# The split of q and k moves from DVE to POOL, attend's sums get a PSUM bank of their own, and every engine's order of work in a tick is written anew

## The chip, the cores and the metric

One core of one Trainium2 chip. The metric is device time in microseconds (us) of one execution; a run's time is the median of its executions. The trace is of one execution taken by the hardware profiler.

## The reference

16 batches of 128 tokens with 128 features go through three attention layers of 16 heads (8 features each) and an MLP:

```python
# layer CROSS0: adaptive layer norm of x and of the context (scale and shift from silu(cond) @ W)
q = (ada(x) @ Wq + bq); k, v = split(ada(ctx) @ Wkv + bkv)
x = x + softmax(q @ k.T / sqrt(8)) @ v @ Wp + bp
# layer SELF1: q, k, v from modulate(ln(x)); the result is gated per batch
x = x + gate_a * (attention(modulate(ln(x))) @ W_proj + b_proj)
# layer CROSS1: q from ln(x), k and v from ln(context); no gate
x = x + attention(ln(x), ln(context)) @ W_cproj + b_cproj
# MLP of 512 hidden features
x = x + gate_m * (gelu(modulate(ln(x)) @ W_mlp1 + b1) @ W_mlp2 + b2)
```

All inputs and outputs are fp32.

## The kernel before, in words

**Units and ticks.** A unit is one batch of one layer: 48 units, 16 for each layer. Four units make a group, 12 groups. Each engine runs a program that is written out in Python: a prologue for group 0, then a loop over ticks (from `FIRST` to `LAST`), and in each tick the steps of several units at different depths of a pipeline. The order of the steps in a tick is fixed by hand (or by a tool that wrote it) for each engine by itself; the engines meet only at semaphores. `front(tick, step)` gives the group whose steps are due at a tick: group g comes at tick 4g + step. So the steps that are done once for a group fall in one tick of every four. This text calls the tick classes T0, T1, T2, T3 by tick modulo 4.

**The steps of a unit.** `scores` (L495): eight bf16 matmuls in two row tiles of 62 rows write four head pairs' scores into `score_ps` (two banks, one buffer); c = 0 and 1 are the two halves of the heads, 0 and 1 in names below. DVE's `row_max` (L930) reduces them to negated maxima. POOL's `split_max` (L1098, L1100) makes two bf16 parts of these, PE's `turn_max` (L502) transposes them, DVE's `copy_max_rows` (L939) takes them to SBUF and SP moves them by two DMAs into the two spare rows of `stack_q` (`move_max`, L343). `keyed_scores` (L518) then computes the scores again, transposed and less their maxima, into `keyed_ps` (one buffer of two banks); ACT's `exponentials` (L737) make `probs`; `attend` (L532), 16 fp32 matmuls with 32 weight columns, multiplies with the values and sums; ACT's `copy_summed` (L745) takes the result out, `turn_summed` (L543) transposes it, DVE's `divide` (L945, L949) divides by the sums, `turn_attn` (L548), ACT's `attn_with_bias` (L754), `project_out` (L555) and DVE's `add_branch` (L960, L963) follow. POOL adds the output bias ahead (`add_out_bias`, L1127) or, in SELF1, multiplies by the gate and adds (`add_gated`, L1148, L1150).

**The steps of a group.** DVE's `norm_stats` (L893, L895), POOL's `inverse_root` (L1082 to L1090), ACT's `normalise_act` (L703) for x and DVE's `normalise` for the context, `transpose_normed` (L459), ACT's `modulate` (L689; plain copies in CROSS1, L682), `project_qk` (L469, one for q and one for k), `project_v` (L478), `copy_values`. q and k are needed as three bf16 parts each, whose sum is the fp32 value. ACT's `first_part` (L717) writes the first part from PSUM, DVE's `leave_rest` (L922) computes PSUM + bias − first part into the fp32 tile `rest`, and POOL's `split_rest` makes the second part by a cast (L1111) and the third by a subtraction (L1113). SP moves the parts by 12 DMAs of 128 KB for each group (`move_parts`, L322) into `stack_q` and `stack_k`; k's parts must have landed before `scores` of the group's first unit, three ticks ahead of the unit's own tick.

**PSUM.** `score_ps` and `keyed_ps` take two banks each; the other four are one ring ("all"), taken in the order that `at_tick` lists. `take` makes PE wait until the use four before has been read.

The MLP's steps (`mlp_up`, `leave_hidden`, `activate_hidden`, `mlp_down`, `add_mlp`) stand at ticks given by tables (`UP_AT`, `GELU_AT`, `DOWN_AT`, `ADD_AT`).

## Time and profile before

| | |
|---|---|
| median of 3 runs | 303.6 us (303.12 to 304.59) |
| the profiled execution | 304.21 us, of it a span of 302.4 us |
| PE matmuls busy | 264.3 us, 87% |
| DVE busy | 220.0 us, 73% |
| ACT busy | 221.8 us, 73% |
| POOL busy | 135.6 us, 45% |
| granted TensorE clock, mean | 0.977 |

The span is the time from the first to the last instruction in the trace; the profiled execution's own time is 1.8 us longer. Busy shares are averages over a start (about 45 us, with loads), the ticks with attention, and a tail (from about 250 us) with the MLP; from 70 to 250 us the granted clock is full.

### The profile page before, as it was taken

What the parts mean: (1) busy time and instruction counts of PE and PEld (TensorE: products, weight loads), DVE (VectorE), ACT (ScalarE), POOL (GpSimd) and SP (SyncE); (2) the same over time, 40 slices, a digit from 0 to 9 for tenths busy, and PEclk for the clock granted to TensorE, in tenths of its full rate; (3) what the DMA queues carried; (4) which work ended last, traced back from release to release, by engine and by line L of the source; (5) the groups of instructions that cost most, each with busy time, mean ns of one, the idle gap of its engine ahead of it and who ended that gap; (6) DMA issues with size and microseconds to landing.
All of it is one profiled execution on the core that took longest, in us unless ns stands there. A gap on an engine that the chain in (4) does not pass through costs nothing.

```text
span 302.4 us, 10123 instructions
## 1 busy us (share of the span) xinstructions
PE 264.3 (87%) x3811; PEld 172.7 (57%) x3811; DVE 220.0 (73%) x452; ACT 221.8 (73%) x399; POOL 135.6 (45%) x285
## 2 busy tenths in 40 slices
PE   2837679989899998989999999999999999978995
PEld 2523446656555665555656666566665555544875
DVE  7776867978778787787887988889878787322323
ACT  5345396886977869778687786976878879899940
POOL 8410924726346163253664735757248153160500
PEclk9975989999999999999999999999999999999999
DMA  6096985235433455432423234232442200000111
GB/s 199 3 208 178 189 189 136 69 89 135 114 108 96 124 131 112 108 112 77 110 69 95 69 95 108 59 95 69 108 108 56 57 5 4 4 2 0 35 54 52
DMA packets 34223, 27.44 MB, mean 91 GB/s; under 512 B 4904, under 2 KB 33920, under 8 KB 34176
## 3 DMA queue, kind: packets, MB, share of 16 engines
q1 hardware_dynamic: 32678, 25.54, 33.3%
q10 hardware_dynamic: 1498, 1.26, 1.7%
q8 instruction: 31, 0.51, 0.7%
q14 instruction: 16, 0.13, 0.1%
HBM read 6.46 MB, written 1.06 MB: 25 GB/s over the span
## 4 chain that ended last, share of the span: by engine, by line
PE 45%; DVE 15%; ACT 13%; POOL 9%; issue 9%; DMA 5%; SPq 3%; ACTq 1%; POOLq 0%; DVEq 0%
PE all_ps L469 8%; PE all_ps L532 8%; DVE neg_max L930 8%; PE score_ps L495 6%; ACT normed L703 4%; PE keyed_ps L518 4%; PE all_ps L543 4%; PE all_ps L459 3%; PE all_ps L563 3%; POOL rstd L1082 3%; PE all_ps L574 2%; PE all_ps L555 2%; ACT parts L717 2%; POOL parts L1113 2%; DMA stack_q<-max_rows 2%
## 5 line engine op out<-in xcount | busy, mean ns | idle before, releaser
L930 DVE TENSOR_REDUCE neg_max<-score_ps 128x8 f32<-128x1024 f32 x96 | 117.0, 1219 | 17.8 <-PE score_ps L495 17.8
L737 ACT ACTIVATE probs<-keyed_ps 128x1024 f32<-128x1024 f32 x96 | 98.2, 1022 | 18.0 <-PE keyed_ps L518 18.0
L532 PE MATMUL all_ps<-probs,values 128*32 128x128 f32 x1536 | 61.7, 280 | 0.3 <-ACT probs L737 0.3
L532 PEld LDWEIGHTS all_ps<-probs,values 128*32 128x32 f32 x1536 | 36.5, 109 | 19.9 <-issue 10.4
L495 PE MATMUL score_ps<-stack_k,stack_q 62*128 62x128 bf16 x768 | 38.6, 221 | 10.6 <-DVE neg_max L930 7.0
L518 PE MATMUL keyed_ps<-stack_q,stack_k 64*128 64x128 bf16 x768 | 38.0, 218 | 2.1 <-DMA stack_q<-max_rows 1.4
L495 PEld LDWEIGHTS score_ps<-stack_k,stack_q 62*128 62x128 bf16 x768 | 22.0, 95 | 30.4 <-DVE neg_max L930 17.3
L1098 POOL CAST max_parts<-neg_max 128x16 bf16<-128x16 f32 x48 | 9.7, 202 | 60.5 <-DVE neg_max L930 60.5
L745 ACT ACTIVATE summed<-all_ps 128x256 f32<-128x256 f32 x48 | 18.2, 380 | 19.1 <-PE all_ps L532 19.1
L469 PE MATMUL all_ps<-normed_t,w_qk 128*128 128x512 f32 x48 | 30.9, 739 | 0.0
L1082 POOL TENSOR_TENSOR rstd<-var_eps,minus_half 128x4 f32<-128x4 f32 x24 | 24.4, 1015 | 12.8 <-DVE var_eps L895 12.7
L518 PEld LDWEIGHTS keyed_ps<-stack_q,stack_k 64*128 64x128 bf16 x768 | 22.7, 94 | 12.8 <-issue 9.3
L1127 POOL TENSOR_TENSOR x_bias<-xs,b_out 128x128 f32<-128x128 f32 x32 | 14.7, 458 | 29.8 <-DVE xs L963 29.5
L1113 POOL TENSOR_TENSOR parts<-rest,parts 128x512 bf16<-128x512 f32 x23 | 26.6, 1155 | 1.8
L703 ACT ACTIVATE normed<-xs,offset,rstd 128x128 f32<-128x128 f32 x56 | 23.0, 485 | 5.9 <-POOL offset L1090 5.7
L922 DVE SCALAR_TENSOR_TENSOR rest<-all_ps,bcol_p,parts 128x512 f32<-128x512 f32 x24 | 17.9, 746 | 12.6 <-ACT parts L717 11.7
L1111 POOL CAST parts<-rest 128x512 bf16<-128x512 f32 x23 | 14.0, 609 | 25.0 <-DVE rest L922 25.0
L543 PE MATMUL all_ps<-ident,summed 128*128 128x128 f32 x96 | 20.9, 300 | 3.9 <-ACT summed L745 3.7
L963 DVE TENSOR_TENSOR xs<-all_ps,x_bias 128x128 f32<-128x128 f32 x32 | 9.2, 287 | 19.0 <-PE all_ps L555 17.9
L717 ACT ACTIVATE parts<-all_ps,bcol_p 128x512 bf16<-128x512 f32 x24 | 16.5, 689 | 7.7 <-PE all_ps L469 7.4
L459 PE MATMUL all_ps<-ident,normed 128*128 128x128 f32 x96 | 16.2, 295 | 5.3 <-DVE normed L907 3.7
L689 ACT ACTIVATE normed_t<-all_ps,mod 128x128 f32<-128x128 f32 x44 | 17.3, 462 | 4.1 <-PE all_ps L459 3.9
(103 smaller groups left out, 403.6 us busy)
## 6 DMA issues: line engine op xcount, KB each, us to landing
stack_q<-parts SPq DMA_DIRECT2D x72, 128.0 KB, 2.5
stack_k<-parts SPq DMA_DIRECT2D x66, 128.0 KB, 2.5
gate<-gate_d SPq DMA_DIRECT2D x16, 128.0 KB, 3.4
stack_q<-max_rows SPq DMA_DIRECT2D x96, 4.0 KB
xs<-in_x_dram SPq DMA_DIRECT2D x4, 256.0 KB, 3.0
cs<-in_ctx_dram SPq DMA_DIRECT2D x4, 256.0 KB, 3.5
out_dram<-xs SPq DMA_DIRECT2D x8, 128.0 KB, 1.8
stack_k<-parts ACTq DMA_DIRECT2D x6, 128.0 KB, 4.0
```

Source lines behind the costliest of these rows:

```text
L459: mm = pe.transpose(ps[:, j * T:(j + 1) * T], normed[:, n, j, :], ident[:, :])
L469: pe.matmul(take("qk"[n], g), w_qk[:, s, n, :], normed_t[:, src, :, :], start=True, stop=True).then_inc(qk_ps, 1)
L495: mm = pe.matmul(score_ps[:, e, a * T:(a + 1) * T], stack_q[rows, g % STACKS, CP * c + a, cols], stack_k[rows, g % STACKS, CP * c + a, col ...
L518: mm = pe.matmul(keyed_ps[:, e, a * T:(a + 1) * T], stack_k[rows, g % STACKS, CP * c + a, cols], stack_q[rows, g % STACKS, CP * c + a, col ...
L532: mm = pe.matmul(ps[QUAD * a:QUAD * (a + 1), c * T:(c + 1) * T], values[:, u // PER % STACKS, u % PER * PAIRS + CP * c + a, 2 * e:2 * e + ...
L543: mm = pe.transpose(ps[:, i * 128:(i + 1) * 128], summed[:, u % 2, i, :], ident[:, :])
L703: ins = act.activation(normed[:, n, j, :], src[:, b0 + j, :], ACT.Identity, bias=offset[:, n, j:j + 1], scale=rstd[:, n, j:j + 1])
L717: act.activation(parts[:, g % 2, n, 0, :], bank("qk"[n], g), ACT.Identity, bias=bcol_p[:, r:r + 1]).then_inc(hi_ready, 1)
L737: act.activation(probs[:, n % 3, :], keyed_ps[:, :, :].rearrange("t e n -> t (e n)"), ACT.Exp, scale=float(D) ** -0.5).then_inc(probs_read ...
L930: dve.tensor_reduce(neg_max[:, u % 2, :, CP * c:CP * (c + 1)], score_ps[:, :, :].rearrange("t e (a k) -> t e a k", k=T), AX.X, ALU.max, ne ...
L1082: ins = pool.tensor_tensor(rstd[:, n, :], var_eps[:, n, :], minus_half[:, :], ALU.pow)
L1113: pool.tensor_tensor(parts[:, g % 2, n, 2, :], rest[:, n, :], parts[:, g % 2, n, 1, :], ALU.subtract).then_inc(done, 1)
```

## The change

Four things change together.

- `leave_rest` goes (except for group 0). ACT's new `whole_part` writes q or k whole, in fp32, into `rest`; it waits until the part splitting of the group before is done. POOL's `split_rest` has four instructions in place of two: cast to the first part (L1127 in the new numbering), subtract it from `rest` in place with fp32 output (L1129), cast to the second (L1133), subtract for the third (L1135). SP waits for `hi_cast` (POOL) where it waited for `hi_ready` (ACT).
- The ring of four banks becomes one bank for `attend` ("way_in") and a ring of three for the rest.
- `max_parts` grows to 128 columns, of which 96 are zeros set once at the start; `turn_max` loads 128 weight columns in place of 32 and writes 128 rows, of which 32 are read.
- Each engine's order within a tick and the ticks of many steps are new; the loop runs from tick −7 to 57 in place of −6 to 56.

```diff
-RINGS = (("all", 4),)
+RINGS = (("way_in", 1), ("all", 3))
-        max_parts = sb("max_parts", [T, 2, 2, 2, PAIRS], BF16)
+        max_parts = sb("max_parts", [T, 2, 4, 2, 2, PAIRS], BF16)
-        FIRST = -6
-        LAST = 57
-        UP_AT = (40, 42, 43, 44, 44, 44, 45, 47, 48, 48, 48, 49, 52, 52, 52, 52)
-        DOWN_AT = (49, 50, 52, 52, 52, 53, 55, 55)
-        GELU_AT = (48, 49, 52)
-        ADD_AT = (51, 51, 52, 52, 52, 53, 53, 53)
+        FIRST = -7
+        LAST = 58
+        UP_AT = (41, 42, 43, 44, 45, 46, 48, 49, 49, 49, 50, 51, 54, 54, 54, 55)
+        DOWN_AT = (48, 51, 52, 53, 56, 56, 57, 57)
+        GELU_AT = (47, 49, 51)
+        ADD_AT = (48, 50, 51, 51, 51, 55, 55, 57)
...
+            def whole_part(g, n):
+                s = layer(g)
+                if g >= 2:
+                    act.wait_ge(split_ready, 2 * (2 * (g - 1) + n - 1))
+                else:
+                    act.wait_ge((q0_split, k0_split)[n], 2)
+                act.wait_ge(qk_ps, 2 * g + n + 1)
+                r = (R_Q, R_K)[n][s]
+                act.activation(rest[:, n, :], bank("qk"[n], g), ACT.Identity,
+                               bias=bcol_p[:, r:r + 1]).then_inc(whole_ready, 1)
...
             def split_rest(g, n):
-                pool.wait_ge(rest_ready, m + 1)
+                if g == 0:
+                    pool.wait_ge(rest_ready, m + 1)
+                else:
+                    pool.wait_ge(whole_ready, m - 1)
+                    if g >= 2:
+                        (q_in_place, k_in_place)[n](pool, g - 2)
+                    pool.tensor_copy(parts[:, g % 2, n, 0, :], rest[:, n, :]).then_inc(hi_cast, 1)
+                    pool.wait_ge(hi_cast, m - 1)
+                    pool.tensor_tensor(rest[:, n, :], rest[:, n, :], parts[:, g % 2, n, 0, :],
+                                       ALU.subtract).then_inc(rest_left, 1)
+                    pool.wait_ge(rest_left, m - 1)
                 pool.tensor_copy(parts[:, g % 2, n, 1, :], rest[:, n, :]).then_inc(done, 1)
```

**The new orders in words.** PE: scores 0, keyed 0, attend 1 of the unit before, turn_attn, [T1: q; T2: v; T0: transposes of x], scores 1, keyed 1, attend 0, turn_max, [T0: transposes of the context; T1: k], turn_summed, project_out. ACT: exponentials 0, copy_summed, [T2: copy_values], attn_with_bias, [T0: modulate x; T1: whole q], exponentials 1, [T0: half of modulate context; T1: whole k; T3: normalise_act], [T0: the other half]. DVE: row_max 0, add_branch (one tick later than before), [T1: normalise context], row_max 1, [T2: norm_stats], copy_max_rows, divide. POOL: out bias or gate, [T1: split of q; T2: split of k], split_max, [T2: inverse_root]. SP: [T2: q's parts; T3: the late parts of k], move_max, [T2: the first parts of k].

**PE, a plain tick and its neighbours, by the order of the instruction streams.** Before, layer CROSS0, from a tick's scores 0 to the next tick's:

```order
L495 MATMUL score_ps<-stack_k,stack_q 128x128 x8
L532 MATMUL all_ps<-probs,values 32x128 x8
L518 MATMUL keyed_ps<-stack_q,stack_k 128x128 x8
L555 MATMUL all_ps<-wp,attn_t 128x128
L502 MATMUL all_ps<-ident_b,max_parts 32x128
L543 MATMUL all_ps<-ident,summed 128x128 x2
L495 MATMUL score_ps<-stack_k,stack_q 128x128 x8
L518 MATMUL keyed_ps<-stack_q,stack_k 128x128 x8
L469 MATMUL all_ps<-normed_t,w_qk 128x512
L548 MATMUL all_ps<-ident,attn 128x128
L532 MATMUL all_ps<-probs,values 32x128 x8
L495 MATMUL score_ps<-stack_k,stack_q 128x128 x8
```

After, the same engine in tick T1 (scores are L498 now, keyed L523, attend L537, turn_attn L553, q and k L472, turn_max L507, turn_summed L548, project_out L560):

```order
L498 MATMUL score_ps<-stack_k,stack_q 128x128 x8
L523 MATMUL keyed_ps<-stack_q,stack_k 128x128 x8
L537 MATMUL way_in_ps<-probs,values 32x128 x8
L553 MATMUL all_ps<-ident,attn 128x128
L472 MATMUL all_ps<-normed_t,w_qk 128x512
L498 MATMUL score_ps<-stack_k,stack_q 128x128 x8
L523 MATMUL keyed_ps<-stack_q,stack_k 128x128 x8
L537 MATMUL way_in_ps<-probs,values 32x128 x8
L507 MATMUL all_ps<-ident_b,max_parts 128x128
L472 MATMUL all_ps<-normed_t,w_qk 128x512
L548 MATMUL all_ps<-ident,summed 128x128 x2
L560 MATMUL all_ps<-wp,attn_t 128x128
```

Both scores now stand directly before keyed scores, attend follows them, and all steps with 128 weight columns stand together after attend; q and k are in one tick.

**ACT, from the end of a T3 to the first exponentials of T1.** Before (SELF1 fronts; the normalising step stood in T2, the modulation in T3):

```order
L703 ACTIVATE normed<-xs,offset,rstd 128x128 x4
L745 ACTIVATE summed<-all_ps 128x256
L737 ACTIVATE probs<-keyed_ps 128x1024
L689 ACTIVATE normed_t<-all_ps,mod 128x128 x2
L737 ACTIVATE probs<-keyed_ps 128x1024
L689 ACTIVATE normed_t<-all_ps,mod 128x128 x2
```

After (exponentials are L755, copy_summed L763, attn_with_bias L772, modulate L694, normalise_act L708):

```order
L708 ACTIVATE normed<-xs,offset,rstd 128x128 x4
L755 ACTIVATE probs<-keyed_ps 128x1024
L763 ACTIVATE summed<-way_in_ps 128x256
L772 ACTIVATE attn_t<-all_ps,bcol 128x128
L694 ACTIVATE normed_t<-all_ps,mod 128x128 x4
L755 ACTIVATE probs<-keyed_ps 128x1024 x2
```

All four modulations now stand ahead of exponentials 1 of T0, where two stood ahead of it and two behind.

**POOL, T1 to T2, after, layer SELF1's fronts** (before, L1111 and L1113 alone made the split, L1098 and L1100 stood ahead of it):

```order
L1127 CAST parts<-rest 128x512
L1129 TENSOR_TENSOR rest<-rest,parts 128x512
L1133 CAST parts<-rest 128x512
L1135 TENSOR_TENSOR parts<-rest,parts 128x512
L1112 CAST max_parts<-neg_max 128x2x8
L1114 TENSOR_TENSOR max_parts<-neg_max,max_parts 128x2x8
L1095 TENSOR_TENSOR rstd<-var_eps,minus_half 128x4
```

The maxima's split and, in T2, the inverse root stand behind the four instructions of the k split.

## Rows read from the trace of the kernel before

**Rows 1.** Timeline, PE, start and us: the scores that open ticks 1, 9, 41, 44.

```profile
46.35 0.47 PE L495 MATMUL score_ps<-stack_k,stack_q 62*128 62x128 bf16 x8
...
86.01 0.40 PE L495 MATMUL score_ps<-stack_k,stack_q 62*128 62x128 bf16 x8
...
239.67 0.40 PE L495 MATMUL score_ps<-stack_k,stack_q 62*128 62x128 bf16 x8
...
253.60 0.40 PE L495 MATMUL score_ps<-stack_k,stack_q 62*128 62x128 bf16 x8
```

**Rows 2.** Timeline, PE weight loads of ticks 16 and 17: start, us, idle before.

```profile
119.56 0.23 PEld L495 LDWEIGHTS score_ps<-stack_k,stack_q 62*128 62x128 bf16 x8 [0.53 <-DVE neg_max L930]
119.89 0.38 PEld L532 LDWEIGHTS all_ps<-probs,values 128*32 128x32 f32 x16
120.47 0.23 PEld L518 LDWEIGHTS keyed_ps<-stack_q,stack_k 64*128 64x128 bf16 x8 [0.20 <-issue]
120.80 0.30 PEld L555 LDWEIGHTS all_ps<-wp,attn_t 128*128 128x128 f32 x2
121.21 0.09 PEld L502 LDWEIGHTS all_ps<-ident_b,max_parts 128*32 128x32 bf16 x1
121.37 0.20 PEld L543 LDWEIGHTS all_ps<-ident,summed 128*128 128x128 f32 x2
121.74 0.23 PEld L495 LDWEIGHTS score_ps<-stack_k,stack_q 62*128 62x128 bf16 x8 [0.17 <-issue]
121.98 0.23 PEld L518 LDWEIGHTS keyed_ps<-stack_q,stack_k 64*128 64x128 bf16 x8
...
125.28 0.30 PEld L469 LDWEIGHTS all_ps<-normed_t,w_qk 128*128 128x128 f32 x2
...
126.56 0.09 PEld L502 LDWEIGHTS all_ps<-ident_b,max_parts 128*32 128x32 bf16 x1
```

**Rows 3.** Timeline, DVE, a T2: maxima 0, then the steps up to maxima 1.

```profile
188.40 1.21 DVE L930 TENSOR_REDUCE neg_max<-score_ps 128x8 f32<-128x1024 f32 x1
189.53 0.28 DVE L960 TENSOR_TENSOR branch<-all_ps,b_out 128x128 f32<-128x128 f32 x1
...
190.34 1.22 DVE L930 TENSOR_REDUCE neg_max<-score_ps 128x8 f32<-128x1024 f32 x1
```

**Rows 4.** Timeline, ACT, a T2: exponentials, then normalise_act.

```profile
171.30 1.02 ACT L737 ACTIVATE probs<-keyed_ps 128x1024 f32<-128x1024 f32 x1 [0.49 <-PE keyed_ps L518]
...
172.47 1.64 ACT L703 ACTIVATE normed<-xs,offset,rstd 128x128 f32<-128x128 f32 x4
```

**Rows 5.** Groups by line and shape: busy us, mean ns; idle before, releaser.

```profile
L1113 POOL TENSOR_TENSOR parts<-rest,parts 128x512 bf16<-128x512 f32 x23 | 26.6, 1155 | 1.8
...
L1082 POOL TENSOR_TENSOR rstd<-var_eps,minus_half 128x4 f32<-128x4 f32 x24 | 24.4, 1015 | 12.8 <-DVE var_eps L895 12.7
...
L922 DVE SCALAR_TENSOR_TENSOR rest<-all_ps,bcol_p,parts 128x512 f32<-128x512 f32 x24 | 17.9, 746 | 12.6 <-ACT parts L717 11.7
...
L689 ACT ACTIVATE normed_t<-all_ps,mod 128x128 f32<-128x128 f32 x44 | 17.3, 462 | 4.1 <-PE all_ps L459 3.9
...
L717 ACT ACTIVATE parts<-all_ps,bcol_p 128x512 bf16<-128x512 f32 x24 | 16.5, 689 | 7.7 <-PE all_ps L469 7.4
...
L1111 POOL CAST parts<-rest 128x512 bf16<-128x512 f32 x23 | 14.0, 609 | 25.0 <-DVE rest L922 25.0
...
L1148 POOL TENSOR_TENSOR branch<-branch,gate 128x128 f32<-128x128 f32 x16 | 7.3, 454 | 9.2 <-DVE branch L960 7.5 <-DMA gate<-gate_d 1.6
...
L895 DVE TENSOR_SCALAR var_eps<-x_stats 128x4 f32<-128x4 f32 x16 | 5.8, 363 | 0.5
...
L1140 POOL TENSOR_TENSOR xs<-xs,gate_b 128x512 f32<-128x512 f32 x4 | 5.3, 1315 | 2.0 <-ACT normed L703 1.8 <-DVE xs L963 0.2
...
L895 DVE TENSOR_SCALAR var_eps<-c_stats 128x4 f32<-128x4 f32 x8 | 1.3, 165 | 0.1
```

**Rows 6.** DMA issues: KB each, median us from issue to landing.

```profile
stack_k<-parts SPq DMA_DIRECT2D x66, 128.0 KB, 2.5
```

More of the change, by code:

```diff
@@ L631, in _ @@
                         mlp_up(n // MLP, n % MLP)
-                if unit(tick):
-                    attend(tick, 0)
+                if tick == 3:
+                    late_modulations()
+                if unit(tick - 1):
+                    turn_summed(tick - 1)
+                if unit(tick - 2):
+                    project_out(tick - 2)
                 if -3 <= tick < 0:
@@ L804, in _ @@
                     modulate(g, 1, True)
-                if unit(tick):
-                    exponentials(tick, 1)
-                g = front(tick, -9)
-                if g is not None:
-                    modulate(g, 0, False)
-                if tick == -1:
-                    clear_values(2)
+                g = attention(front(tick, -7))
+                if g is not None:
+                    whole_part(g, 1)
+                if tick == -2:
+                    clear_values(2)
+                g = front(tick, -9)
+                if g is not None and g > 1:
+                    normalise_act(g, 0)
+                for n in range(MLP * B // PER):
+                    if UP_AT[n] == tick:
+                        leave_hidden(n)
                 if tick in GELU_AT:
@@ L1046, in _ @@
                         add_mlp(n)
-                g = attention(front(tick, -8))
-                if g is not None:
-                    leave_rest(g, 0)
+                if unit(tick - 1):
+                    divide(tick - 1)
         @block.gpsimd
```

236 lines of the change are left out of this document (114 added, 122 removed).

## The prediction, made before the result was known

> **What bounds the kernel now.** The busy shares name PE (87%, DVE and ACT 73% each), but a share says nothing of order, so I went on to the timeline. Ticks 1 to 40 take 239.67 − 46.35 = 193.3 us, 4.83 a tick or 19.3 a group; ticks 9 to 40 take 153.7, 19.2 a group; 41 to 43 take 13.9; from the start of tick 44 to the end of the span are 48.8 us [rows 1]. PE's weight loads show what a step costs from its start to the next one's: scores to attend 0.33, attend to keyed 0.58, keyed to project 0.33, project to turn_max 0.41, turn_max to turn_summed 0.16, turn_summed to scores 0.37, scores to keyed 0.24, and 0.53 of idle time that DVE ended [rows 2]. Where 62- or 64-row loads follow 32-column ones or the reverse, a gap of 0.20 marked "issue" stands ahead of the next load; between scores and keyed there is none. k costs 1.28 − 0.41 = 0.87 more than projection alone [rows 2]. So a tick of PE is 3.6 without extras, and with q, k, v (0.87 each) and one set of transposes (0.5) a group is 14.3 + 3.1 = 17.4 us; the other 1.8 are waits. DVE has the second clock: maxima 0 takes 1.13 until the next step starts, the steps up to maxima 1 another 0.81 [rows 3], maxima 1 1.13 again, and about 0.95 pass around it (scores 0.4, signals, scores of the next half can't start before the maxima of this one are out): 4.0 for a plain tick. **Two clocks, PE and DVE, alternate**, and ACT lies just behind.
>
> **The change, part by part.** All sums go against the span of 302.4.
>
> *PE's order.* Both scores are now followed by keyed scores (0.24), then attend (0.33), then 128-column work (0.58): a tick is 0.24 + 0.33 + 0.58 + 0.25 (one transpose, where two take 0.37) + 0.24 + 0.33 + 0.58 + 0.12 (turn_max without its own gap) + 0.17 + 0.31 = 3.15 in place of 3.6. The group's PE work falls from 17.4 to 15.7. That is the gain on offer, 1.7 a group; what of it arrives is set by the others. Turn_max's 96 more columns cost nothing: it was 0.16 from start to start [rows 2] and waits at no wider load; if the wider load costs, its bounds are 0 and one 0.23 us matmul a tick.
>
> *DVE.* It loses leave_rest, 2 × 0.75 = 1.5 a group [rows 5]. add_branch now falls into the time in which DVE waits for scores 1. A plain tick on DVE: 0.44 until maxima 0, 1.23 with its end, 0.06 back to PE; scores 1, 0.44, 1.13, copy and divide 0.61, maxima 0 1.23: 3.75 from scores 1 to scores 1, where it was 4.0.
>
> *POOL.* Four steps in place of two, twice a group: cast 0.69 with its wait, subtraction 1.16, again both: 3.65 for q and as much for k, 3.6 more a group [rows 5]. The subtraction with fp32 output is not in the trace: its ends are 1.16 (bf16 output) and 1.32 (all fp32) [rows 5]; I take 1.16, since one input stays bf16.
>
> *ACT.* whole_part costs what first_part did, 0.69 [rows 5]. But the order matters: T3 ends with normalise_act (1.54 to 1.64, [rows 4]); T0 then has exponentials 0 (0.92), copy 0.3, attn_t 0.36, **all four modulations** (4 × 0.35 = 1.4, from L689's 0.46 that overlap by a quarter [rows 5]) and only then exponentials 1. PE's keyed 0 of T1 waits for those.
>
> *One group, worked out* (zero: keyed 0 in T1; attention in CROSS layers, fronts of SELF1):
> - T1: attend 0.33, turn_attn 0.9, q 1.15, scores 1 at 2.05, keyed 1 2.25, attend 2.6, turn_max 3.15, k 3.3, turn_summed 4.1, next scores 0 at 4.6. Whole q is ready at 3.0, whole k at 5.1.
> - T2: scores 0 4.6, v 6.0, scores 1 6.85. DVE: maxima 1 7.3 to 8.4, norm_stats to 9.55, copy and divide 10.15, maxima 0 of T3 to 11.4. POOL: q split 3.0 to 6.65, maxima 7.1, k split to about 11.3, maxima to 12, inverse root (1.0 [rows 5] and two short steps) to 13.1.
> - T3: scores 0 8.55, but scores 1 only at 11.45 (1.2 us of waiting for DVE), next scores 0 13.15; ACT: exponentials 1 12.1 to 13.0, normalise 13.0 to 14.6.
> - T0: exponentials 0 14.55, copy, attn_t, modulations 16.15 to 17.55, exponentials 1 to 18.55; **keyed 0 of the next T1 at 18.6**, though PE could have had it at 17.4.
>
> So a group takes 18.6, not 15.7: two waits, for DVE's norm_stats in T3 and for ACT in T0 and T1, take most of what PE's order frees. Where POOL also has add_gated (2 × 0.45 [rows 5], ticks 19 to 34), its inverse root ends 0.7 later, ACT's normalising with it: 19.3 a group. Fronts of CROSS1 copy in 0.5 in place of 1.4: 18.45 with gates, 17.85 without. Ticks 9 to 40: 2 × (18.65 + 19.3 + 18.45 + 17.85) = 148.5 against 153.7: **−5.2**. Ticks 1 to 8 (39.7 [rows 1]), with context norms still to do: −0.7. Ticks 41 to 43: −0.3.
>
> *PSUM.* With three banks, turn_summed waits for the use three before; in the working above that use is always read in time, except project_out in T0, which waits for the modulations (17.65) and so for the same ACT chain. Nothing is added.
>
> *SP and DMAs.* In T3 the late parts of k are issued from 12.9 to 14.8 and the maxima of T1 behind them to 16.1; k's parts land 2.5 later [rows 6], about 17, and are needed at 18.0 to 18.4, the maxima at 18.6. Hidden, with about 1 us of cover.
>
> *Start.* Group 1's split of q (3.65) now stands ahead of POOL's first maxima, and normalise_act ahead of the first exponentials, while the weights are issued sooner. No row shows this; I bound it by −1 (loads sooner) and +2 (one more normalisation in the chain, 1.64 [rows 4]) and take +0.5.
>
> *Tail.* From tick 44 ACT is close to saturated, and one group's modulations (1.4) move from before tick 44 to behind it, with the first Gelu ahead of the last unit's sums: **+1.4**, ends 0 and +4 (all that ACT now does after the last exponentials and did before).
>
> Sum: −5.2 − 0.7 − 0.3 + 0.5 + 1.4 = −4.3: a span of 298.1, an execution of 299.9 against 304.2; the runs' median lies 0.6 below that execution, so **299.3 us**.
>
> **The rivals.**
>
> *A, PE's order pays in full.* If ACT's chain in T0 is shorter than I make it (the modulations and exponentials overlap), DVE is the next limit: 3.75 to 4.8 a tick, worked out as above 17.3 a group. Ten groups × 1.9 = 19 less, tail and start as above: 287; halfway, 293. For it speaks PE's 87%; against it the two waits above. 18% for a time under 297.
>
> *B, the freed time is given back at both ends.* Start +2, tail +4: with −6.2 in the ticks the change is near zero, 303.5. 15%. A measurement of this kernel can tell about 0.5% from no change.
>
> *C, POOL becomes the gate: slower.* POOL has 14 of 18.6 us to do in a group of a SELF1 layer, and its chain q split, maxima, k split, maxima, root ends where PE (turn_max of T3 at 12.55, cover 0.5) and ACT (normalise at 13.0) want it. Each 0.1 us by which a step of the split is longer delays both by 0.4. The upper price (1.32) gives +0.3 to +0.6; DVE's var_eps takes 0.36 on x, beside POOL's splits, and 0.17 on the context [rows 5], so DVE too is held up by POOL, in T2, where it is on the path. A hold-up of one whole subtraction (1.16) there is +0.8. From +0.5 a group on (10 groups: +5) the gain is gone; at +0.8, with the tail, it is 307. 24%.
> The Trainium skill (SBUF — State Buffer, "Who interferes with whom") says that a DVE instruction in a two-port mode, or with two SBUF inputs against a POOL instruction that reads SBUF, fully blocks or is blocked for the whole instruction. By that rule norm_stats' last step and the context's normalising would wait for up to one POOL step each, which is case C; the trace agrees in direction (0.36 against 0.17) and shows 0.2 us so far, not a whole step.
>
> *D, the change isn't what it says*: the split would stay on DVE. The order listing shows no leave_rest after the prologue; left out.
>
> **How the numbers follow.** Forecast case (297 to 302) 43%, A 18%, B 15%, C 24%. Faster by over 0.5% (under 302.1): 0.61; within 0.5%: 0.15; slower: 0.24. The likeliest case by itself: 296 to 302. The range leaves out A's full gain and the worst of C: 290 to 307.
>
> **What would show it.** In the new profile: keyed scores directly behind scores without an issue gap, DVE's waits for scores 1 holding add_branch; groups of 18 to 19 us; PE waiting for the maxima in T3 for about 1 us and for the exponentials in T1 for about 1 us; POOL's busy time up by 11 × 3.6 = 40 us to about 175, DVE's down by 17 to about 203. Wrong would be: the starts of T1 17.3 apart (A), PE's turn_max or ACT's normalising waiting for POOL (C), or keyed scores waiting for the DMA of the maxima.

## The result, and the profile after

The changed kernel takes **313.35 us** (312.46 to 314.02, 4 runs) against 303.52 us (303.12 to 304.59, 4 runs): a ratio of **1.032, 95% interval 1.029 to 1.036**. Forecast were 299.3 us and a range of 290 to 307. The profiled execution took 312.94 us, its span is 311.1 us, 8.7 more than before. Executions over 1.5% longer than the fastest of their kernel are left out of the ratios but not of the medians and ranges, and the profiles of a_same, a_tail2, a_maxfirst and b_both below are of such executions.

The page of the changed kernel, its busy times (us, share of the span, instructions) and the granted clock in 40 slices of the span (tenths of full speed):

```profile
PE 256.3 (82%) x3811; PEld 173.8 (56%) x3811; DVE 208.7 (67%) x430; ACT 218.8 (70%) x399; POOL 172.8 (56%) x330
...
PEclk9985979959999999899999999999799999977999
```

POOL's busy time is near the forecast one (172.8 against about 175), DVE's is 5.7 above it (208.7 against about 203), and the new subtraction costs the 1.16 us assumed, from the groups by line and shape (busy us, mean ns of one | idle before):

```profile
L1135 POOL TENSOR_TENSOR parts<-rest,parts 128x512 bf16<-128x512 f32 x23 | 26.6, 1156 | 1.8
L1129 POOL TENSOR_TENSOR rest<-rest,parts 128x512 f32<-128x512 f32 x22 | 25.4, 1157 | 1.8
```

So no new operation was mispriced; what was wrong is when things happen, and what DVE's steps cost while POOL works beside them. PE's timeline (start, us), the scores that open ticks 1, 9, 17, 41 and 44, to be laid beside [rows 1]:

```profile
48.20 0.40 PE L498 MATMUL score_ps<-stack_k,stack_q 62*128 62x128 bf16 x8 [1.53 <-DMA stack_k<-parts]
...
89.08 0.40 PE L498 MATMUL score_ps<-stack_k,stack_q 62*128 62x128 bf16 x8
...
128.23 0.40 PE L498 MATMUL score_ps<-stack_k,stack_q 62*128 62x128 bf16 x8 [0.92 <-issue]
...
243.89 0.40 PE L498 MATMUL score_ps<-stack_k,stack_q 62*128 62x128 bf16 x8
...
257.67 0.40 PE L498 MATMUL score_ps<-stack_k,stack_q 62*128 62x128 bf16 x8
```

| stretch | before | forecast change | after | measured change |
|---|---|---|---|---|
| up to tick 1 | 46.35 | +0.5 | 48.20 | +1.85 |
| ticks 1 to 8 | 39.66 | −0.7 | 40.88 | +1.2 |
| ticks 9 to 40 | 153.66 | −5.2 | 154.81 | +1.15 |
| ticks 41 to 43 | 13.93 | −0.3 | 13.78 | −0.15 |
| tick 44 to the end | 48.80 | +1.4 | 53.43 | +4.6 |
| span | 302.4 | −4.3 | 311.1 | +8.7 |

The groups from tick 9 on take 19.4, 19.7, 20.9, 19.3, 18.6, 18.6, 19.7 and 18.7 us. The forecast group of 18.6 is there, but only three of eight reach it. Where the others lose time shows in the windows of the trace (the window and its length; busy us of PE, PEld, DVE, ACT and POOL, each with its instructions; then the granted clock as a share of 2.4 GHz, DMA share, GB/s):

```profile
60.00:69.00 9.00, 8.42 (x114) 6.38 (x114) 4.80 (x12) 5.68 (x12) 3.89 (x12) 0.62 0.41 114
130.00:133.00 3.00, 3.00 (x21) 1.15 (x19) 0.09 (x1) 1.70 (x3) 0.00 (x0) 0.52 0.26 72
218.00:223.00 5.00, 5.00 (x78) 3.58 (x78) 3.36 (x7) 4.08 (x8) 2.91 (x9) 0.66 0.41 108
276.00:283.00 7.00, 4.24 (x17) 3.92 (x18) 0.42 (x1) 4.57 (x11) 1.44 (x2) 0.56 0.00 0
```

In four stretches that ran at 2.4 GHz before, TensorE was granted 1.2 GHz for a few microseconds. Each follows waits of PE: for DVE and SP around ticks 0 to 3, for scores 0 (0.92 us) and for the DMA of the maxima (1.02 us) in tick 17, for DVE's attn and maxima around tick 35, for ACT in the tail. The two middle ones lie in the groups of 20.9 and 19.7. That the waits caused the falls is read from their order in time; no run separates the two.

**SP's queue.** The wait in tick 17, and what SP and DVE had done for it (timelines of PE, SP, DVE):

```profile
129.65 0.40 PE L523 MATMUL keyed_ps<-stack_q,stack_k 64*128 64x128 bf16 x8 [1.02 <-DMA stack_q<-max_rows]
...
114.23 5.11 SPq L325 DMA_DIRECT2D stack_q<-parts  x6
119.39 0.59 SPq L335 DMA_DIRECT2D gate<-gate_d  x1
120.07 1.37 SPq L346 DMA_DIRECT2D stack_q<-max_rows  x2
121.55 4.67 SPq L325 DMA_DIRECT2D stack_k<-parts  x6
126.27 0.59 SPq L335 DMA_DIRECT2D gate<-gate_d  x1
126.96 1.37 SPq L346 DMA_DIRECT2D stack_q<-max_rows  x2
...
121.89 0.20 DVE L957 COPY max_rows<-all_ps 32x128 bf16<-32x128 bf16 x1
```

The maxima were in SBUF at 122.09. SP came to them at 126.96, because from 114.23 on it issued 18 DMAs in a row, 14.1 us with gaps of at most 0.12 us between the rows, and PE needed them at 128.63.

**DVE beside POOL.** Timeline around tick 35, POOL's subtraction and DVE's var_eps, and two waits of PE behind it:

```profile
214.91 1.16 POOL L1129 TENSOR_TENSOR rest<-rest,parts 128x512 f32<-128x512 f32 x1
...
215.31 0.79 DVE L913 TENSOR_SCALAR var_eps<-x_stats 128x4 f32<-128x4 f32 x1
...
216.77 0.33 PE L553 MATMUL all_ps<-ident,attn 128*128 128x128 f32 x1 [0.84 <-DVE attn L967]
...
217.90 0.40 PE L498 MATMUL score_ps<-stack_k,stack_q 62*128 62x128 bf16 x8 [0.80 <-DVE neg_max L948]
```

var_eps, 0.17 us when alone, ends at 216.10, and POOL's subtraction at 216.07: DVE was held until POOL's step was over. That is the rule of the Trainium skill (SBUF — State Buffer, "Who interferes with whom"), and in this instance the trace agrees with it. It is the longest hold of this step in the running ticks: of the eight var_eps of x in ticks 9 to 41, four took 0.17 us, three 0.38 to 0.57 and this one 0.79, where the kernel before had 0.43 or 0.44 in all eight. Of the two waits behind it only the first is its work (0.84 us where the other groups have 0.2 to 0.6); the second, for the maxima of T3, is 0.8 us in every group.

**The tail.** Timeline of the changed kernel, ACT, PE and DVE behind the last exponentials:

```profile
272.61 1.02 ACT L755 ACTIVATE probs<-keyed_ps 128x1024 f32<-128x1024 f32 x1
273.53 1.64 ACT L708 ACTIVATE normed<-xs,offset,rstd 128x128 f32<-128x128 f32 x4
...
275.18 1.28 ACT L792 ACT_TABLE_LOAD   x1
...
276.47 2.19 ACT L792 ACTIVATE hidden<-hidden 128x512 f32<-128x512 f32 x4
278.57 0.36 ACT L763 ACTIVATE summed<-way_in_ps 128x256 f32<-128x256 f32 x1
...
278.76 3.76 PE L579 MATMUL all_ps<-w,hidden 128*128 128x128 f32 x16 [2.89 <-issue]
282.31 1.72 PE L568 MATMUL all_ps<-c_rep,w 128*128 128x512 f32 x2
283.86 0.38 PE L548 MATMUL all_ps<-ident,summed 128*128 128x128 f32 x2
...
288.09 0.29 DVE L981 TENSOR_TENSOR xs<-all_ps,x_bias 128x128 f32<-128x128 f32 x1 [3.02 <-PE all_ps L560]
```

The last unit's sums wait for the first Gelu and its table load on ACT, and then on PE for the first down projection and an up projection behind it (3.8 and 1.7 us), at half clock. The last add_branch comes 15.5 us behind the start of the last exponentials, where it was 7.2 (278.60 − 271.37), and the end 38.5 us behind them in place of 31.0.

### The profile page after: what moved, and what is told of

Read it like the earlier page. It is cut to its first block, busy times and chain, and to the rows that moved or that the text cites. A ratio compares the mean times of both kernels' runs of the same rounds, so it can differ in the third digit from the quotient of the medians.

```text
span 311.1 us, 10127 instructions
## 1 busy us (share of the span) xinstructions
PE 256.3 (82%) x3811; PEld 173.8 (56%) x3811; DVE 208.7 (67%) x430; ACT 218.8 (70%) x399; POOL 172.8 (56%) x330
## 3 DMA queue, kind: packets, MB, share of 16 engines
q10 hardware_dynamic: 1498, 1.26, 1.7%
## 4 chain that ended last, share of the span: by engine, by line
PE 35%; POOL 19%; DVE 12%; ACT 11%; issue 9%; SPq 6%; DMA 5%; ACTq 0%; POOLq 0%; DVEq 0%
PE way_in_ps L537 5%; DVE neg_max L948 5%; PE all_ps L472 5%; PE all_ps L579 5%; POOL rest L1129 4%; POOL parts L1135 4%; PE score_ps L498 4%; SPq L325 4%; ACT normed L708 4%; PE all_ps L568 3%; PE keyed_ps L523 3%; PE all_ps L462 3%; DMA stack_k<-parts 3%; POOL parts L1133 2%; POOL parts L1127 2%
## 5 line engine op out<-in xcount | busy, mean ns | idle before, releaser
L755 ACT ACTIVATE probs<-keyed_ps 128x1024 f32<-128x1024 f32 x96 | 98.4, 1025 | 31.1 <-PE keyed_ps L523 30.8
L537 PE MATMUL way_in_ps<-probs,values 128*32 128x128 f32 x1536 | 63.2, 283 | 0.0
L498 PE MATMUL score_ps<-stack_k,stack_q 62*128 62x128 bf16 x768 | 39.6, 225 | 21.2 <-DVE neg_max L948 15.4
L498 PEld LDWEIGHTS score_ps<-stack_k,stack_q 62*128 62x128 bf16 x768 | 22.6, 96 | 42.9 <-DVE neg_max L948 22.8
L537 PEld LDWEIGHTS way_in_ps<-probs,values 128*32 128x32 f32 x1536 | 37.1, 110 | 10.4 <-issue 0.6
L523 PE MATMUL keyed_ps<-stack_q,stack_k 64*128 64x128 bf16 x768 | 38.7, 220 | 3.7 <-DMA stack_q<-max_rows 2.3
L523 PEld LDWEIGHTS keyed_ps<-stack_q,stack_k 64*128 64x128 bf16 x768 | 25.6, 96 | 7.4 <-DMA stack_q<-max_rows 3.5
L472 PE MATMUL all_ps<-normed_t,w_qk 128*128 128x512 f32 x48 | 29.2, 702 | 0.0
L708 ACT ACTIVATE normed<-xs,offset,rstd 128x128 f32<-128x128 f32 x56 | 23.0, 482 | 8.1 <-POOL offset L1103 8.1
L1135 POOL TENSOR_TENSOR parts<-rest,parts 128x512 bf16<-128x512 f32 x23 | 26.6, 1156 | 1.8
L1129 POOL TENSOR_TENSOR rest<-rest,parts 128x512 f32<-128x512 f32 x22 | 25.4, 1157 | 1.8
L722 ACT ACTIVATE rest<-all_ps,bcol_p 128x512 f32<-128x512 f32 x22 | 15.1, 687 | 13.6 <-PE all_ps L472 13.5
L963 DVE RECIPROCAL r_sum<-all_ps 128x16 f32<-128x16 f32 x48 | 11.9, 248 | 16.4 <-PE all_ps L548 16.4
L1127 POOL CAST parts<-rest 128x512 bf16<-128x512 f32 x22 | 13.4, 611 | 15.8 <-ACT rest L722 15.8
L553 PE MATMUL all_ps<-ident,attn 128*128 128x128 f32 x48 | 16.0, 333 | 4.7 <-DVE attn L967 4.3
L548 PE MATMUL all_ps<-ident,summed 128*128 128x128 f32 x96 | 19.1, 281 | 0.0
L462 PEld LDWEIGHTS all_ps<-ident,normed 128*128 128x128 f32 x96 | 11.5, 154 | 12.9 <-ACT normed L708 7.4
```

The costliest lines, as they stand in the source:

```text
L462: mm = pe.transpose(ps[:, j * T:(j + 1) * T], normed[:, n, j, :], ident[:, :])
L472: pe.matmul(take("qk"[n], g), w_qk[:, s, n, :], normed_t[:, src, :, :], start=True, stop=True).then_inc(qk_ps, 1)
L498: mm = pe.matmul(score_ps[:, e, a * T:(a + 1) * T], stack_q[rows, g % STACKS, CP * c + a, cols], stack_k[rows, g % STACKS, CP * c + a, col ...
L523: mm = pe.matmul(keyed_ps[:, e, a * T:(a + 1) * T], stack_k[rows, g % STACKS, CP * c + a, cols], stack_q[rows, g % STACKS, CP * c + a, col ...
L537: mm = pe.matmul(ps[QUAD * a:QUAD * (a + 1), c * T:(c + 1) * T], values[:, u // PER % STACKS, u % PER * PAIRS + CP * c + a, 2 * e:2 * e + ...
L708: ins = act.activation(normed[:, n, j, :], src[:, b0 + j, :], ACT.Identity, bias=offset[:, n, j:j + 1], scale=rstd[:, n, j:j + 1])
```

## The experiments

Ratios are to the kernel before on the same chip. The columns "tick 1", "9 to 41" and "end" (us) are from the profiled execution: the start of tick 1, the time from tick 9 to tick 41, and the time from the start of the last exponentials to the end of the span.

| kernel | median us (range, runs) | ratio, 95% interval | tick 1 | 9 to 41 | end |
|---|---|---|---|---|---|
| before | 303.52 (303.12 to 304.59, 4) | 1 | 46.4 | 153.7 | 31.0 |
| changed | 313.35 (312.46 to 314.02, 4) | 1.032, 1.029 to 1.036 | 48.2 | 154.8 | 38.5 |
| a_same | 311.64 (309.31 to 314.18, 4) | 1.023, 1.016 to 1.030 | 48.0 | 156.3 | 37.8 |
| b_ring | 313.89 (312.84 to 314.79, 4) | 1.035, 1.032 to 1.039 | 46.4 | 161.4 | 31.5 |
| b_split | 322.04 (320.98 to 323.03, 4) | 1.060, 1.054 to 1.067 | 47.2 | 167.5 | 31.0 |
| b_both | 325.93 (321.92 to 330.17, 4) | 1.064, 1.057 to 1.071 | 48.1 | 170.8 | 31.5 |
| a_dve | 321.56 (320.02 to 324.41, 4) | 1.060, 1.051 to 1.069 | 45.9 | 163.4 | 37.8 |
| a_maxfirst | 319.58 (317.36 to 324.29, 4) | 1.050, 1.042 to 1.058 | 49.0 | 163.2 | 38.6 |
| a_gates | 309.30 (305.94 to 309.98, 4) | 1.016, 1.009 to 1.022 | 48.1 | 151.2 | 37.7 |
| a_start | 311.11 (310.11 to 313.18, 4) | 1.027, 1.022 to 1.032 | 46.3 | 157.5 | 37.8 |
| a_tail | 317.27 (311.43 to 319.49, 4) | 1.047, 1.038 to 1.056 | 47.8 | 152.8 | 40.1 |
| a_tail2 | 309.68 (306.66 to 312.38, 4) | 1.016, 1.009 to 1.023 | 47.8 | 155.3 | 35.4 |
| a_short | 311.49 (310.15 to 315.38, 4) | 1.024, 1.018 to 1.029 | 46.8 | 154.8 | 38.9 |
| a_gt | 308.87 (305.97 to 310.80, 4) | 1.016, 1.011 to 1.021 | 48.0 | 150.0 | 36.8 |
| a_all | 306.98 (305.43 to 308.45, 6) | 1.012, 1.009 to 1.016 | 46.2 | 151.5 | 36.7 |
| a_var | 309.31 (307.45 to 310.25, 4) | 1.017, 1.012 to 1.022 | 47.1 | 153.3 | 36.7 |
| a_tail3 | 306.45 (303.75 to 308.19, 10) | 1.007, 1.004 to 1.011 | 46.3 | 152.9 | 36.4 |
| a_best | 307.67 (306.12 to 309.45, 6) | 1.013, 1.009 to 1.017 | 46.2 | 153.2 | 34.9 |
| a_stats | 304.70 (303.22 to 308.28, 12) | 1.005, 1.002 to 1.008 | 46.0 | 150.5 | 34.8 |
| a_stats_short | 300.25 (299.27 to 304.56, 4) | 0.986, 0.981 to 0.992 | 45.7 | 148.0 | 36.4 |

a_same is the changed kernel once more, the measure for the scatter.

> The changed kernel once more, unaltered, as the measure for the three beside it on the same chip: 312 to 315 us. If its times spread by more than 1% here, the stretches in which PE is granted half its clock fall differently from run to run, and differences of 1% between variants say little.

It scatters by 1.6%, the kernel before by less than 1% beside it. In which ticks the clock falls differs between profiles (in tick 17 it fell in a_same and did not in a_tail, whose queue is the same), so where medians differ by about 1% the text goes by the stretches of the profiles, less any stretch at half clock that lies in them.

### The parts of the change alone, in the old order

**b_split**: ACT's whole_part and POOL's four steps put into the kernel before, leave_rest taken out.

> The kernel before with one part of the change only: ACT writes q and k whole, POOL makes all three parts, DVE none; every order, bank and table as before. Theory N (the new orders of work lose the time, at the tail, in SP's queue and at the start, and PE's waits then cost clock): 302 to 305 us, since DVE gets 16 us free and POOL goes from about 130 to 170 us busy off the path. Rival C (POOL is the gate and holds DVE up): 307 us or more, with PE waiting for maxima parts and row maxima or var_eps several tenths longer.

**b_ring**: the rings and the 128 columns alone.

```diff
-RINGS = (("all", 4),)
+RINGS = (("way_in", 1), ("all", 3))
```

> The kernel before with two small parts of the change only: attend's sums in a bank of their own with three banks for all else, and the turn of the maxima with 128 columns. Theory N: both cost nothing, 302.5 to 305 us. Rival R (three banks make PE wait for readers, or the wider load costs its 0.23 us a tick): 307 us or more, with waits of turn_summed, v or the transposes for DVE's rest or ACT.

**b_both**: both of these.

> The kernel before with all of the change but the new orders: ACT writes q and k whole and POOL makes the three parts, attend's sums have a bank of their own, the maxima turn with 128 columns; every engine's order and the tables are the old ones. If the bank of its own costs 10 us in the old order only because k's bank is freed late by DVE's subtraction (which ACT's whole copy does sooner), the two prices do not add: 320 to 324 us. If they are independent, 331 to 335.

Theory N fell in the first two. The waits of b_split (whole span) and b_ring (us 86 to 246): what waited for what, us in total, times, longest.

```profile
ACT normed L705 <- POOL offset L1099: 20.5, 11, 6.5
...
PE all_ps L504 <- POOL max_parts L1109: 10.2, 11, 2.7
PE all_ps L545 <- ACT summed L760: 10.1, 12, 1.3
```

```profile
PE all_ps L546 <- DVE rest L925: 11.1, 8, 1.4
```

In the old order POOL's longer split stands in front of the maxima and of the root, and PE and ACT wait for both: the gate of rival C. And with three banks turn_summed gets the bank of k, which DVE's subtraction has not read yet: 1.4 us in each group, 8 times. The two prices, 18.5 and 10.9 us by the medians, do not add (29.4): by the ratios b_both is 6.4% slower than the kernel before and b_split alone 6.0%, with overlapping intervals. The bank's own price is small there but not nothing: turn_summed still waits for ACT's whole_part to read k's bank (from the waits of b_both, "all_ps L548 <- ACT rest L722", 5.9 us in 9 waits, at most 0.7 each). b_both has all of the change but the new orders and tables, and is 6.4% slower; the changed kernel is 3.2% slower. So the new orders do give back about 10 us, half of what the other parts cost in the old ones. Whether the 128 columns have a share was not tried apart; no row of b_ring waits for that load.

### The new order with the old split

**a_dve**: the changed kernel with first_part, leave_rest and the two-step split back. The edit in DVE's program, in short:

```diff
...
+                if g is not None:   # q: front(tick, -7), behind maxima 1; k: front(tick, -6), behind maxima 0
+                    leave_rest(g, n)
...
```

> The changed kernel with the split put back: ACT rounds the first part, DVE leaves the rest (q's behind maxima 1 of T1, k's behind maxima 0 of T2), POOL makes two parts; the new orders, the bank of its own and the tables stay. Theory N: still 310 to 314 us, since tail, SP queue and start are as they are; the DMA waits for k and the maxima shrink by at most 2 us because parts are ready some 2 us sooner. Rival C: 305 us or less, since POOL's 40 us are gone.

Slower still. PE waits for turn_attn's bank until DVE has left k's rest (11.5 us in 9 waits of "all_ps L552 <- DVE rest L939"), the same clash as in b_ring, at the place that I chose for that step. So it shows that the new order needs the bank freed by ACT, but says nothing clean on the order by itself. The changed kernel's own order with the old ring of four was not run: project_out of T1 would then be the fourth use behind attend's sums and would wait for them to be read, while the second half of attend stands behind it in PE's order, so PE would wait for itself.

### SP's queue

**a_maxfirst**: move_max ahead of k's late parts and the gates.

> The changed kernel with SP's move of the maxima ahead of k's late parts and of the gates in every tick (q's parts stay ahead of it). Theory Q (it is the queue's order that makes keyed scores of T1 wait for the maxima): the waits of keyed scores for the DMA of the maxima in T1 go, the half-clock stretch at 130 us goes, 309.5 to 311.5 us. Rival S (SP issues too much in T3, whatever the order): k's last parts land about 1.3 us later, scores 0 of T1 wait for them instead, 313 to 316 us.

Rival S, and worse than it said. In T1 scores 0 now wait, 0.8 to 1.8 us in seven of nine groups (in the profiled execution, which took 324.3 us against a median of 319.6; the trace names no releaser, but what stands ahead of these scores is the wait for k's parts). Turning the queue around only moves the wait.

**a_gates**: four gates in T0 in place of one a tick.

```diff
-                if 0 < tick - 2 <= B:
-                    spread_gate(tick - 3)
                 if unit(tick + 2):
                     move_max(tick + 2)
+                if tick in (4, 8, 12, 16):
+                    for b in range(tick - 4, tick):
+                        spread_gate(b)
```

> The changed kernel with the sixteen DMAs that spread the gates issued four at a time in T0 of ticks 4, 8, 12 and 16, behind the maxima, in place of one in each of the ticks 3 to 18 ahead of the maxima. Theory Q (SP's queue in T2 and T3 is what is late): the maxima of T3 and k's last parts go out 0.6 to 1.2 us sooner in ticks 5 to 18, T1's waits for their DMA there shrink to nothing, groups 9 to 20 take 18.6 to 19.0 in place of 19.4 to 20.9, and the time is 2 to 4 us less. Rival: no change beyond 1 us, since in T3 the queue waits for POOL's split of k.

Theory Q holds. SP's timeline of the same place, and the window around 130 us:

```profile
118.69 1.37 SPq L346 DMA_DIRECT2D stack_q<-max_rows  x2
120.17 3.82 SPq L325 DMA_DIRECT2D stack_k<-parts  x6
124.09 3.53 SPq L346 DMA_DIRECT2D stack_q<-max_rows  x4
127.66 1.82 SPq L335 DMA_DIRECT2D gate<-gate_d  x4
```

```profile
130.00:133.00 3.00, 3.00 (x56) 1.95 (x50) 1.98 (x5) 2.25 (x3) 2.15 (x3) 1.00 0.49 125
```

The maxima go out at 124.09 in place of 126.96, the clock stays whole, and groups 9 to 20 take 18.7, 18.7 and 18.5 us in place of 19.4, 19.7 and 20.9 (a_same: 19.5, 19.9, 20.9). The ratios of a_gates and a_same (1.016 and 1.023) overlap in their intervals. The twelve ticks 9 to 20 are clearer: 56.0 us in a_gates and 56.0 to 57.0 in the seven later kernels that have this edit, against 60.0 and 60.3 in the changed kernel and a_same. In a_tail, where the queue is the changed kernel's and the clock did not fall in tick 17, they take 58.3: of the 4 us, about 2 are waits and about 2 the clock.

### Start

**a_start**: on DVE, `normalise(2, 1)` behind both maxima of unit 1.

> The changed kernel with one step moved on DVE: the context's normalising of group 2 stands behind both maxima of unit 1 in place of ahead of them. Theory P (this step takes 3.8 us beside POOL's new steps in place of 1.1, and PE's first scores wait for it): tick 1 starts 2 to 3 us sooner, at 45.5 to 46.5, and the time falls by 1.5 to 3 us against the changed kernel's 309 to 315. Rival (the loads or POOL's chain set the start): tick 1 stays at 48.

Theory P: tick 1 at 46.3. In the changed kernel this step took 3.76 us (1.26 before, 1.11 where nothing held it) and kept the first maxima until 35.14. Ticks 1 to 4 take 20.4 in place of 22.0, since the clock's fall at 62 us is gone too. But the median moved within the scatter only: ticks 9 to 12 and 17 to 20 had half-clock stretches of their own in the profiled run.

### Tail

**a_tail**, **a_tail2** and **a_tail3** change the tables alone (the last on top of the gates and the start).

```diff
-        DOWN_AT = (48, 51, 52, 53, 56, 56, 57, 57)
-        GELU_AT = (47, 49, 51)
+        DOWN_AT = (50, 51, 53, 53, 53, 54, 56, 56)   # a_tail
+        GELU_AT = (49, 50, 52)
+        DOWN_AT = (51, 51, 52, 52, 53, 54, 56, 56)   # a_tail2
+        GELU_AT = (49, 51, 52)
+        DOWN_AT = (51, 51, 51, 52, 53, 54, 56, 56)   # a_tail3
+        GELU_AT = (49, 50, 52)
```

> The changed kernel with other tables for the MLP's steps (the first down projection in tick 50 in place of 48, the first Gelu in tick 49 in place of 47, the rest about as before the change, one tick later), so that turn_summed and project_out of unit 47 no longer stand behind the first Gelu and the first down projection. Theory N: the last add_branch comes 6 to 8 us after the start of the last exponentials in place of 15.5, and the end comes 4 to 6 us sooner: 307.5 to 309.5 us. Rival (the tail is bound by ACT's sum of work after the last exponentials, whatever its order): 312 to 314 us.

> The changed kernel with other ticks for the MLP's steps alone: two more up projections before the last exponentials, the first Gelu behind attn_t of unit 47, the first down projection and the ups of the third quarter behind project_out of unit 47, the second Gelu behind the last normalisation. Theory T (the tail's loss is the place of the first Gelu and the first down projection, and, once these are moved, of the second Gelu ahead of the last normalisation): last add_branch 6 to 8 us after the start of the last exponentials, the last normalisation 11 to 12, the end 30 to 32: 6 to 8 us less than the changed kernel, 305 to 308 us. Rival (ACT's sum of work sets the tail): the end stays 36 us or more behind the last exponentials and the time over 311.

> The changed kernel with the three edits, but the MLP's steps in a third set of ticks: the second Gelu directly behind the first and the third quarter's hidden copies, ahead of the last normalisation, and three down projections ahead of PE's last transposes. Theory T2 (PE has 20 us of MLP work behind the first Gelu and must not idle there): 32 to 34.5 us from the last exponentials to the end in place of 36.7, 303 to 305.5 us. Rival: the last normalisation comes 2 to 4 us later and takes the gain back: 36 us or more.

The times with a plus are counted from the start of the last exponentials. In a_tail the last add_branch came at +8.7 us, near the 6 to 8 expected, but the end came later (40.1 us) and the median is 317.3: the second Gelu had slipped ahead of the last normalisation, which came at +20.0 (changed kernel +18.5, before +10.9). a_tail2 has the two at +6.5 and +11.0 and ends at +35.4, 3 us better; a_tail3, +6.6 and +12.9, ends at +36.4 with a half-clock stretch inside (its twin a_best at +34.9). None comes back to 31.0. ACT is busy for 22.2 of the changed kernel's 38.5 us and was for 18.8 of 31.0, so ACT's sum alone does not set the tail. PE is busy for 30.1 in place of 25.7, at a mean clock of 0.91 in place of 1.00, and idle for 8.4 in place of 5.3: the 7.5 us are about 3 of idling (one gap of 2.9 stands ahead of the first down projection) and over 4 of steps that are slower or more. What the deeper pipeline itself costs here (normalising and modulating group 14 behind the last exponentials, 1.6 and 1.5 us) I can't separate from the tables.

### Sums, and POOL's chain

**a_gt** (gates, a_tail2) and **a_all** (these and a_start):

> The changed kernel with the gates' DMAs four at a time in T0, and with the second set of ticks for the MLP's steps. If the two causes are apart, their gains add: ticks 9 to 41 in 151 us, 35 us from the last exponentials to the end, 304 to 308 us in all. If not, about 309 as with either alone.

> The changed kernel with three edits: the gates in T0, the second set of ticks for the MLP's steps, and the context's normalising of group 2 behind the maxima of unit 1. Theory N (the change loses at start, in SP's queue and in the tail, and these three are most of it): 302 to 306 us, no slower than the kernel before by more than 1%. Rival (the loss is spread over the ticks, by POOL's load or by the clock): 308 us or more.

The edits add in the profiles (a_gt: ticks 9 to 41 in 150.0; a_all: tick 1 at 46.2, ticks 9 to 41 in 151.5); a_gt's median is 308.9, just over its 304 to 308, and a_all's of 307 lies between theory and rival, mostly for the tail.

**a_var** (a_all with var_eps on POOL) and **a_best** (a_var with a_tail3's tables):

> The changed kernel with the three edits (gates in T0, second set of MLP ticks, context's normalising of group 2 behind the maxima of unit 1) and var_eps made by POOL, just ahead of its power, in place of by DVE, for groups 2 and later. Theory P (DVE's var_eps is held for what is left of POOL's subtraction, 0.80 us in place of 0.17, in T2, where the maxima of T3 and the divide wait behind it): 0.3 to 0.6 us a group less, ticks 9 to 41 in 147 to 149.5 us in place of 151.5, 302 to 305 us. Rival: the 0.2 us more in POOL's chain to the root delays ACT's normalising and T0, no gain or 1 us more: 306 to 309.

> All edits that the runs so far point to in one kernel: gates in T0, context's normalising of group 2 behind the maxima, var_eps on POOL, third set of MLP ticks. If the gains add: ticks 9 to 41 in 148 to 149.5, the end 33 us behind the last exponentials, 298 to 302 us, faster than the kernel before. Rival (half-clock stretches come back somewhere, or the tail stays): 303 to 307.

The rival, in both. The waits of a_all and then of a_var, us 86 to 238 (total us, times, longest):

```profile
PE all_ps L554 <- DVE attn L968: 3.6, 8, 0.8
PE all_ps L463 <- ACT normed L709: 3.5, 7, 0.6
...
ACT normed L709 <- POOL offset L1106: 2.2, 7, 0.4
```

```profile
ACT normed L711 <- POOL offset L1116: 8.6, 8, 1.6
PE all_ps L465 <- ACT normed L711: 8.2, 7, 1.5
```

What PE no longer waits for in T2 (attn) it waits for in T0, where POOL's root comes too late for ACT's normalising.

**a_stats**: a_tail3, and DVE's norm_stats of x in T3 behind maxima 0.

```diff
-                g = front(tick, -10)
-                if g is not None and g > 1:
-                    norm_stats(g, 0)
+                g = front(tick, -9)            # behind row_max(tick + 3, 0)
+                if g is not None and g > 1:
+                    norm_stats(g, 0)
```

> The changed kernel with the gates in T0, the context's normalising of group 2 behind the maxima, the third set of MLP ticks, and one more edit: DVE's norm_stats of x stands in T3 behind maxima 0 in place of in T2 ahead of the copy of the maxima and the divide. Theory P2 (POOL's chain splits, maxima, root sets T0, and DVE's stats only have to be there when POOL comes to its root): the waits of turn_attn for attn in T2 and of scores 1 for the maxima in T3 (0.8 us each) go, while ACT's normalising waits for POOL as long as before; ticks 9 to 41 in 148 to 151 us, 302 to 305 us in all. Rival (var_eps now meets POOL's last subtraction, or PE's gain in T2 and T3 is waited for in T0): no gain, 306 us.

Theory P2, and the best correct version: 304.7 us, ticks 9 to 41 in 150.5, groups of 18.4 to 19.1. It still does not beat the kernel before. Its waits, us 85 to 236:

```profile
ACT normed L709 <- POOL offset L1106: 10.8, 8, 1.9
...
PE all_ps L463 <- ACT normed L709: 6.1, 8, 0.8
...
PE all_ps L508 <- POOL max_parts L1117: 2.7, 4, 0.9
```

**a_short** and **a_stats_short**: POOL's first subtraction left out, in the changed kernel and in a_stats.

```diff
-                    pool.tensor_tensor(rest[:, n, :], rest[:, n, :], parts[:, g % 2, n, 0, :],
-                                       ALU.subtract).then_inc(rest_left, 1)
```

> The changed kernel with POOL's first subtraction left out for groups 1 to 11 (the second and third parts are then made from the whole value, so the products are not those of the reference): 2.3 us of POOL less in a group, k's and q's late parts ready 1.2 and 2.3 us sooner. Rival C (POOL's load, by the chain to the DMAs or by holding DVE up, is the gate): 6 us or more less than the changed kernel, 307 or under, with DVE's var_eps and the context's normalising back near 0.2 and 1.1 us. Theory N (PE, DVE and ACT set the ticks, and the loss lies in tail and clock): 309 to 313.

> The kernel of a_stats with POOL's first subtraction left out for groups 1 to 11 (the products are not the reference's). The same leaving-out gave nothing in the ticks of the changed kernel itself (154.8 us both). If POOL's chain is what sets a group once the other waits are gone: the 2.3 us a group come through until PE's or DVE's own sum binds, ticks 9 to 41 in 141 to 147 us in place of 150.5, 294 to 300 us, with the transposes of T0 no longer waiting 0.8 us for ACT's normalising. Rival (PE and DVE alternate and set 18.6 to 19 us themselves): 149 us or more, 302 to 305 us.

In the changed kernel POOL's load is at most a small part of the loss: without 25 us of it the median is 311.5, where a_same on the same chip has 311.6 (tick 1 comes 1.4 sooner and ticks 1 to 4 take 19.8, the start again). That ticks 9 to 41 take 154.8 both times is chance, though, and the expectation of a_stats_short read too much into it: a_short has a stretch at half clock of its own at the start of tick 9,

```profile
88.00:90.00 2.00, 2.00 (x18) 1.08 (x19) 0.00 (x0) 1.76 (x3) 0.45 (x1) 0.50 0.31 86
90.00:92.00 2.00, 2.00 (x22) 0.80 (x20) 0.34 (x1) 0.69 (x1) 0.08 (x1) 0.50 0.07 18
```

and its first group takes 22.1 in place of 19.4. The seven groups behind it take 132.7 in place of 135.4, of which 1.6 are the group of tick 17, where the clock did not fall. Once the queue, the start and DVE's places are mended, the same leaving-out counts for more: 148.0 in place of 150.5 in ticks 9 to 41, 0.3 us a group, and 300.3 in place of 304.7 by the medians (ratios 0.986 and 1.005, intervals apart). That is 4 to 6 us, and it takes the kernel below the one before. ACT's normalising still waits 6.2 us for POOL in eight groups there, PE 4.9 us for DVE's maxima and 4.1 for the normalising; which of the three engines would bind next is not shown. In a_var and a_stats it is POOL's chain that ends T0, by ACT's waits of 8.6 and 10.8 us for it; in a_all these are 2.2.

## Why the prediction was wrong, point by point

- **"Hidden, with about 1 us of cover" (SP and DMAs)** is the step that failed worst. I counted SP's work in T3 alone: the late parts from 12.9 to 14.8 and the maxima to 16.1, against 18.6. From the start of tick 13, a T1, at 108.49 the trace has, in my us of a group, k's DMAs from 13.1 to 17.7 and the maxima from 18.5 to 19.8, with PE there at 20.1. Left out were k's first parts and the gate, which stand behind the maxima of T2, and which q's six DMAs in turn push back. The cover was below zero, which my own last paragraph named as the sign of an error. Price in ticks 9 to 20, by a_gates: 4 us, the fallen clock included, of the 6.35 by which ticks 9 to 40 missed the forecast.
- **No term for the clock.** Every wait was priced by its own length. Two of 0.9 and 1.0 us in tick 17 were followed by a stretch at 1.2 GHz, and the group took 20.9 in place of 18.5 (a_gates).
- **Start, +0.5 with ends −1 and +2**: +1.85, inside the ends, but ticks 1 to 8 gave +1.2 more in place of −0.7. I had POOL's order in mind; the cause is DVE's normalising beside POOL, 3.76 us in place of 1.26; moved, it gives the 1.85 back (a_start, tick 1 at 46.3).
- **Tail, +1.4 with ends 0 and +4**: +4.6. I named the first Gelu's place and did not follow it up: it holds copy_summed, PE puts a down projection in front of the last turn, and 15.5 us pass where 7.2 did.
- **A group of 18.6 us**: met, in the changed kernel in three groups of eight and in a_gates, within 0.2, in five of eight, but in part by luck, since it is made up otherwise. PE's waits in the two groups of 18.6 (us 168.3 to 205.6: total us, times, longest):

```profile
PE score_ps L498 <- DVE neg_max L948: 1.6, 2, 0.8
PE all_ps L462 <- ACT normed L708: 1.1, 2, 0.6
PE all_ps L553 <- DVE attn L967: 0.9, 2, 0.4
```

  The wait for DVE in T3 was 0.8 us where I said 1.2. The second wait of the forecast, 1.2 us for the exponentials behind the modulations in T1, isn't there: from tick 9 to tick 41 no keyed scores wait for exponentials. In its place PE waits 0.6 for ACT's normalising in T0 and 0.4 for attn in T2. Waits of 1.8 leave 16.8 us for PE's own steps, where I had 15.7. The step that was wrong is thus the path through T0: the transposes wait for the normalising, which stands ahead of all modulations. So copies in their place gain nothing, and the terms 18.45 and 17.85 of CROSS1 were too low: a_all has 19.0 and 18.6 for the one, 19.0 and 18.8 for the other, 2.8 us more in four groups.
- **PSUM, "nothing is added"**, and turn_max nothing: right for the new order. The reason is the change's own: ACT frees k's bank at once. With DVE's subtraction in its place the bank costs 11 us (b_ring); in the old order it still waits for ACT (b_both).
- **The rivals.** C had the sign and both mechanisms in it (var_eps held for a whole step, the root late), and with 24% was given too little; but its price in the changed kernel is small (a_short), and in a_stats, where the other losses are mended, 4 to 6 us in all, 0.3 us a group in the ticks (a_stats_short). B had the places, start and tail, and both went further than its bounds or to them. The loss is B's ends plus a queue, which none of the four cases contained.

## What to carry to other kernels

Walk through the queue that issues the DMAs as you do through an engine: every transfer of a period, with its issue time and the waits in front of it, from the busiest stretch on. And price a wait of TensorE that is new by more than its length, in a kernel whose trace has stretches at half clock behind such waits. Such a stretch in one of two profiles can hide a gain or feign one, as in a_short: look at the clock of each stretch before you compare two. A new order and a new place for the work may be bound to each other: tried alone, the bank and the split cost 11 and 18.5 us, and with the new orders both together 9.8, so an ablation of one part says little on its worth in the whole.
